# Attention loop: one step's values weighed behind each step's scores, in place of two steps' weighing in one run

## The reference, cut to what matters

```
energy = jnp.einsum('bhqd,bhkd->bhqk', q, k) / jnp.sqrt(jnp.float32(D))
energy = jnp.where(mask_input == 0, jnp.float32(-1000000000.0), energy)
attn = jax.nn.softmax(energy, axis=-1)
context = jnp.einsum('bhqk,bhkd->bhqd', attn, v)
```

## Time and profile before

| | |
|---|---|
| Median of 3 runs (lowest to highest) | 899.23 us (899.07 to 899.9) |
| The profiled execution: its own time | 899.97 us |
| Its span, first to last instruction | 898.2 us |
| PE busy | 870.7 us, 97% of the span |
| DVE, ACT busy | 606.6 us, 479.8 us |
| The loop of the change | from about 89 us to 511 us of the span |

### The profile page before, as it was taken

How to read it: one execution, slowest core, us unless ns; L and a number is a source line. 1 busy time by engine, 2 the same in 40 slices (tenths; PEclk the granted TensorE clock), 3 DMA queues, 4 the chain that set the end, 5 groups by cost and what they waited for, 6 DMA issues and landing times.

```text
span 898.2 us, 15321 instructions
## 1 busy us (share of the span) xinstructions
PE 870.7 (97%) x6029; PEld 518.3 (58%) x6031; DVE 606.6 (68%) x1060; ACT 479.8 (53%) x973; POOL 141.4 (16%) x144
## 2 busy tenths in 40 slices
PE   8899999999999999999999999999999999999998
PEld 4556444444556665555545587654884784656745
DVE  6988877778885556888872589977724228379352
ACT  5452666777775566777779852214411310668221
POOL 7353111111000000000000260010100006345100
PEclk9999999999999999999999999999999999999999
DMA  9989564453523112222613440084645705000000
GB/s 353 301 262 221 132 169 113 118 165 112 129 66 90 36 36 72 72 71 72 191 37 136 169 178 1 1 292 138 227 188 186 282 22 167 1 1 1 1 1 24
DMA packets 55083, 108.50 MB, mean 121 GB/s; under 512 B 5409, under 2 KB 38177, under 8 KB 49825
## 3 DMA queue, kind: packets, MB, share of 16 engines
q1 hardware_dynamic: 52832, 103.29, 37.5%
q10 hardware_dynamic: 2176, 4.19, 1.7%
HBM read 93.58 MB, written 13.89 MB: 120 GB/s over the span
## 4 chain that ended last, share of the span: by engine, by line
PE 82%; DVE 11%; ACT 2%; DMA 2%; issue 1%; POOL 1%; SPq 0%; DVEq 0%; ACTq 0%
PE psum L2049 14%; PE psum L2031 13%; PE psum L1998 11%; PE psum L2448 6%; PE psum L2476 6%; PE psum L1961 5%; PE psum L2580 5%; PE psum L1971 4%; DVE arena L1528 3%; PE psum L2213 3%; PE psum L2645 2%; PE psum L2630 2%; PE psum L2200 2%; DVE arena L1281 1%; PE psum L2669 1%
## 5 line engine op out<-in xcount | busy, mean ns | idle before, releaser
L1281 DVE TENSOR_REDUCE arena<-psum 128x1 f32<-128x1024 f32 x256 | 300.9, 1218 | 97.3 <-PE psum L1998 96.8
L849 ACT ACTIVATE arena<-psum 128x512 f32<-128x512 f32 x512 | 263.1, 602 | 67.0 <-PE psum L2031 65.9
L1998 PE MATMUL psum<-arena 120*128 120x512 bf16 x512 | 151.7, 379 | 5.7 <-DVE arena L1281 3.4
L2031 PE MATMUL psum<-arena 120*128 120x256 bf16 x1024 | 154.8, 274 | 1.8 <-ACT arena L849 0.5
L2049 PE MATMUL psum<-arena 128*32 128x256 f32 x2048 | 137.0, 385 | 0.0
L2031 PEld LDWEIGHTS psum<-arena 120*128 120x128 bf16 x1024 | 80.5, 97 | 96.2 <-ACT arena L849 36.7
L2049 PEld LDWEIGHTS psum<-arena 128*32 128x32 f32 x2048 | 53.4, 109 | 74.2 <-ACT arena L849 30.7
L711 POOL TENSOR_TENSOR arena<-arena 128x512 bf16<-128x512 f32 x34 | 41.4, 1219 | 158.3 <-DVE arena L1267 140.4
L1971 PE MATMUL psum<-arena 128*128 128x256 f32 x256 | 63.2, 384 | 0.0
L1998 PEld LDWEIGHTS psum<-arena 120*128 120x128 bf16 x512 | 48.7, 98 | 23.4 <-DVE arena L1281 11.9
L1961 PE MATMUL psum<-arena 128*128 128x512 f32 x128 | 60.9, 603 | 0.0
(11 more groups left out here) (269 smaller groups left out, 1024.3 us busy)
## 6 DMA issues: line engine op xcount, KB each, us to landing
arena<-mask SPq DMA_DIRECT2D x12, 1024.0 KB, 6.1
kparts<-arena SPq DMA_DIRECT2D x32, 384.0 KB, 3.4
arena<-kparts SPq DMA_DIRECT2D x32, 384.0 KB, 4.6
arena<-ctxT SPq DMA_DIRECT2D x16, 512.0 KB, 5.9
arena<-kparts SPq DMA_DIRECT2D x32, 256.0 KB, 5.1
arena<-ctx SPq DMA_DIRECT2D x2, 4096.0 KB, 17.3
arena<-ctxT ACTq DMA_DIRECT2D x8, 512.0 KB, 8.2
arena<-kparts SPq DMA_DIRECT2D x32, 128.0 KB, 5.5
```

The lines of the kernel that those rows point to most:

```text
L849: nc.scalar.activation(PR[step % 4][:, pair * CH:(pair + 1) * CH], exp_bank(step, pair), ACT.Exp, scale=DH ** -0.5)\
L1281: nc.vector.tensor_reduce(MX[g % 2][:, col:col + 1], unit_banks(n).rearrange("p b n -> p (b n)"), AX.X, ALU.max).then_inc(s_maxed, 1)
L1998: last = nc.tensor.matmul(out, q, KST[g % 2][0:ROWS, quarter, j, half * CH:(half + 1) * CH], start=True, stop=not masked, skip_group_check ...
L2031: last = nc.tensor.matmul(heads[:, u, :], KST[gg % 2][0:ROWS, kc // 8, j, kc % 8 * P:(kc % 8 + 1) * P], QST[0:ROWS, b, G * g + j, :], star ...
```

## The change

The weighing moves from the end of the iteration (two steps in one run, behind both steps' scores and behind keys, values and contexts) into the step: after step s has issued its scores and its units, step s - 2 is weighed. Before, steps 2m - 2 and 2m - 1 were weighed at the end of iteration m; now 2m - 2 stands between the iteration's two steps, and 2m - 1 behind the second step, ahead of keys, values and contexts.

```diff
@@ -2086,15 +2086,14 @@
                             turned_scores(step, masked)
                             for n in range(units_by(step - 1), units_by(step)):
                                 scores(n, masked)
+                            if step >= 2:
+                                weigh_values(step - 2)
                         if keys_at(gg, m):
                             project_keys(1, *keys_at(gg, m))
                         if gg and m == 1:
                             turn_context(gg - 1)
                         if values_after(gg, m):
                             project_values(1, *values_after(gg, m))
-                        if gg or m:
-                            weigh_values(KC * gg + 2 * m - 2)
-                            weigh_values(KC * gg + 2 * m - 1)
                         if gg + 1 == GROUPS and m == KC // 2 - 1:
                             pe.wait_ge(on["w_quantised"], 1)
                             pe.wait_ge(norm_step, 3 * GPB)
```

## The result

The changed kernel takes **931.7 us** (931.06 to 932.45, 4 runs) for 899.57 before: 32.1 us or 3.5% slower, ratio 1.0354 with a 95% interval of 1.0342 to 1.0367. The forecast was 928.0, range 919 to 936. The profiled executions differ by 31.1 us of span, 929.3 for 898.2.

The account below looks back on a forecast made before the run. PE was taken to bound the loop. Runs +29.8, units -3.3, keys +3.8 and scores -1.5 sum to +28.8 us: 928.8 from the profiled execution, 928.0 from the median, range 919 to 936.

Parts of the forecast that it names:

- Point 1: Weighing on PE: 255 runs for 128, 127 more at 0.235 us each, +29.8 us.
- The forecast's floor of 0.195: Least price in us of an added weighing run, its two empty passages alone; +24.8 us in all.
- Point 2: Early PE stalls at units behind DVE, 4.7 us: four small covered, two large keep about 0.67 each; -3.3 us.
- Point 3: Scores right behind keys: PE stalls 0.27 us for an exponential, 14 times, +3.8 us; none behind values.
- Point 4: Scores stalled at the ring once units are gone: a weighing between covers them, less 0.3 for a copy; -1.5 us.
- Point 5: End of the loop: ACT gets slack, PE pays the whole 0.235 us per iteration; no further term.
- A: Rival: the holes around weighings are waits, so the change is faster, as low as 868 us; chance 0.03.
- B: Rival: added passages are hidden by weight loads during streaming, so no change, 898.2 us; chance 0.02.
- C: Rival: a short weighing run switches more cheaply, half the price remains, 913 us; chance 0.07.
- D: Rival: ACT becomes late, whole-exponential stalls behind keys and cost at the loop's end, 939 us; chance 0.08.

Follow-up runs that it names:

- runs 3 and 4: Kernel before plus one extra bf16 matmul ahead of each odd step's unit, 109 times: weights 32 columns wide in one (933.67 us), 128 in the other (912.11 us).
- run 2: Changed kernel with keys, contexts and values back ahead of the second weighing, still one step weighed per run: 924.09 us, ratio 1.0268.

## Why the prediction was right, and by how much it missed

**The bound and the mechanism** held: PE sets the loop's pace, and what the new order makes PE do beside its matmuls is the loss.

**Point 1, the runs** (+29.8): 255 runs, each 0.57 plus the 0.095 ahead of it, as read from a first and a last round; the chain's two steps came out at the forecast's 3.08. The extra matmuls of runs 3 and 4 give 0.198 for the two passages alone; with the slower first round, 0.03, that is 0.228, close to the 0.235. The forecast's floor of 0.195 was worked out too low: its last round of 0.33 less 0.21 of streaming leaves 0.12 empty and not 0.10.

**Point 2, units that waited for DVE** (-3.3): the four small stalls are gone, the two large ones show 0.42 idle each, so 0.59 for the forecast's 0.67. -3.5.

```profile
119.13 0.61 PE L1998 MATMUL psum<-arena 120*128 120x512 bf16 x2 [0.42 <-DVE arena L1281]
...
128.40 0.61 PE L1998 MATMUL psum<-arena 120*128 120x512 bf16 x2 [0.42 <-DVE arena L1281]
```

**Point 3, keys ahead of scores** (+3.8): by the starts in the trace, 13 stalls of 0.25 and not 14 of 0.27, 3.2; and one of 1.08, where keys and the first context's turn stand together and scores come right behind both, which I had overlooked:

```profile
167.14 0.39 PE L2031 MATMUL psum<-arena 120*128 120x256 bf16 x2 [0.92 <-ACT arena L822]
```

Together 4.3. No stall followed behind values, as forecast.

**Point 4, scores that waited for exponentials** (-1.5): over the starts of the trace these stalls fell by about 2.9, as parts of the stalls at the turns of the maxima went too. The wait for the group's copy added 0.19 for the 0.3 estimated: that weighing starts 0.73 behind the scores' start, where 0.54 is usual there.

**The term that was missing.** Point 3 costed the scores behind a projection, but not the projection behind a weighing. By the starts, the loop from its first scores to the matmul behind its last weighing takes 453.2 us for 421.5, 31.7 more; the profiled spans differ by 31.1, as the work ahead of the loop was 0.6 shorter in that execution. 29.8 - 3.5 + 4.3 - 2.9 = 27.7. Of the missing 4.0, 3.1 are a second hole, 0.10 behind the first matmul of each of the 31 projections that now follow a weighing; about 1 more is the same hole at its smaller size in contexts and scores (last section). The page shows the projections' part in their own lines, 1.2 for L1961 and 1.8 for L1971, and it goes back when the projections stand behind units again (run 2). One of them, before and after:

```profile
293.43 1.89 PE L1971 MATMUL psum<-arena 128*128 128x256 f32 x8
```

```profile
295.04 1.99 PE L1971 MATMUL psum<-arena 128*128 128x256 f32 x8
```

That is a tenth of a microsecond in each. The sum had the passage from narrow to wide at one hole wherever it stands; into an fp32 projection it costs two. Two errors partly cancel, then: about 4 us of second holes that the sum left out, and in point 4 a saving that it put 1.4 too small. The centre came out 3.7 us low.

**Point 5** held: near the end, PE again has every microsecond and paid in full, while ACT gets through 52 instructions in 29 us where it had 57:

```profile
512.00:541.00 29.00, 29.00 (x318) 12.40 (x314) 11.89 (x14) 27.83 (x52) 0.00 (x0) 1.00 0.35 122
```

**The rivals.** A and B fell with runs 3 and 4 and with the chain; C with the starts, 0.31 from a run's last matmul to the scores behind one, two and four steps alike; D did not come about, the stall behind keys stayed at a quarter microsecond but for the one of 1.08. By the Trainium skill's rule that a change of tiling mode drains TensorE (page "TensorEngine Tiling (Array Packing)", section Key Properties) the trace and the extra matmuls agree, with about 0.1 us empty each way; the 166 ns taken from "TensorE: Matmul & The Clock Gate", section Single matmul latency, as an estimate of its price would be 0.33 for a pair of passages, and the measured 0.198 decides.

## What to carry to other kernels

When PE is the bound, count how often its program goes between weights of different width, and price a passage from distances between starts in the trace, not from idle times or the names of the waits view. Group narrow matmuls as far as the buffers of the engines beside PE allow: here two steps in a run beat one step by 32 us and four by 20. And cut a run apart only where PE stands still anyway; ten cuts at such places gained 3.3 us, 127 everywhere lost 32, of which 24 remain when the projections keep their place.

## What the runs showed of the hardware that was not expected

A passage into fp32 weights of 128 columns leaves a second hole behind the first matmul. In the changed kernel a projection of keys stands behind a weighing at 163.80, and its four matmuls span 1.98; before, behind a unit, 1.88. PEld and PE, after:

```profile
163.79 0.30 PEld L1961 LDWEIGHTS psum<-arena 128*128 128x128 f32 x2 [0.41 <-issue]
163.80 1.98 PE L1961 MATMUL psum<-arena 128*128 128x512 f32 x4
```

And before:

```profile
175.56 0.31 PEld L1961 LDWEIGHTS psum<-arena 128*128 128x128 f32 x2 [0.21 <-issue]
175.67 1.88 PE L1961 MATMUL psum<-arena 128*128 128x512 f32 x4
```

Behind a unit the first weights load 0.11 ahead of the first matmul; behind a weighing load and matmul start together, and the matmul after the first comes 0.10 later than it would. By the starts of the trace the delay goes with the length of that load: 0.01 in the scores (a load of 0.10), 0.05 in the turn of a context (0.14), 0.10 in keys and values (0.19).

A change of width is not needed for it. In the kernel before, at 479.93, PE had waited for ACT between scores and the turn of a context, both 128 wide; load and matmul start together there too, and the two matmuls last 0.44, where behind a unit, with the load ahead, they last 0.39:

```profile
435.50 0.39 PE L2059 MATMUL psum<-arena 128*128 128x128 f32 x2
...
479.93 0.20 PEld L2059 LDWEIGHTS psum<-arena 128*128 128x128 f32 x2 [1.06 <-ACT arena L849]
```

So the second hole seems to belong to a load that could not run ahead, and the passage between widths is one way to get there. No run tried the load's length by itself.
